# The experts' second layer with the weighted hidden values as stationary operand, in a vision tower on Trainium2

## What is computed

```python
logits = tokens @ router_w.T            # 8 experts
rw, re = top_k(softmax(logits), 2)      # two gates a token
rw = rw / rw.sum(-1)
out = tokens
for e in range(8):
    h = gelu(tokens @ w1[e] + b1[e])    # 64 -> 64
    y = h @ w2[e] + b2[e]               # 64 -> 64
    out = out + combine[:, e:e+1] * y
h = layernorm(out)
```

## Time and profile before

| | value |
|---|---|
| median of 3 runs | 2671.2 us |
| profiled execution | 2679.64 us, span 2677.9 us |
| TensorE matmul busy, whole span | 2344.8 us (88%) |
| VectorE | 1966.0 us (73%) |
| ScalarE | 1902.9 us (71%) |
| GpSimd | 1825.7 us (68%) |
| mean granted clock of TensorE | 0.97 |
| second stage | from about 2236 us to the end, 442 us |
| L1170 (down), matmuls | x512, 592 to 644 ns each |
| L1180 (turn_back), matmuls | x128, median 273 ns |

### The profile page before, as it was taken

One profiled execution on the slowest core, in us unless ns is written; L12 is line 12 of the kernel. 1 busy time (PEld: TensorE's weight loads), 2 busy tenths in 40 slices (PEclk: granted clock), 3 DMA queues, 4 the chain that ended last, 5 costly groups with the idle time before them and its releaser, 6 DMA issues. The chain is left out here.

```text
span 2677.9 us, 92863 instructions
## 1 busy us (share of the span) xinstructions
PE 2344.8 (88%) x32965; PEld 1114.5 (42%) x32965; DVE 1966.0 (73%) x4552; ACT 1902.9 (71%) x4717; POOL 1825.7 (68%) x1949
## 2 busy tenths in 40 slices
PE   1788888888888888888888888888888877999997
PEld 0344444444444444444444444444444443333332
DVE  4577777777777777777777777777777766898987
ACT  3777777777777777777777777777777764555554
POOL 3678877787787787777777877877877861222323
PEclk9999999999999999999999999999999996999999
DMA  4333333333333333333333333333332200000001
GB/s 83 73 65 65 65 65 65 64 65 64 65 65 65 64 65 65 64 65 65 65 65 64 65 65 64 65 65 62 67 65 60 54 2 1 21 20 20 20 21 27
DMA packets 573723, 147.95 MB, mean 55 GB/s; under 512 B 573440, under 2 KB 573440, under 8 KB 573440
## 3 DMA queue, kind: packets, MB, share of 16 engines
q1 hardware_dynamic: 573440, 143.52, 27.4%
HBM read 135.09 MB, written 8.39 MB: 54 GB/s over the span
## 5 line engine op out<-in xcount | busy, mean ns | idle before, releaser
L709 POOL TENSOR_TENSOR pv<-vs,aw 128x512 f32<-128x512 f32 x512 | 534.9, 1076 | 431.8 <-DVE aw L923 431.8
L840 DVE TENSOR_TENSOR kqs<-ps,qqT 128x512 f32<-128x512 f32 x512 | 352.0, 688 | 317.8 <-PE ps L390 313.9
L385 PE MATMUL ps<-xb,w_ckv 64*64 64x512 f32 x2048 | 570.4, 635 | 8.3 <-DVE kqs L840 5.1
L591 ACT ACTIVATE xd<-xb 128x512 f32<-128x512 f32 x512 | 576.1, 1151 | 0.0
L390 PE MATMUL ps<-xb,w_ckv 64*64 64x512 f32 x2048 | 570.6, 635 | 0.0
L573 ACT ACTIVATE sqs<-ps 128x512 f32<-128x512 f32 x512 | 309.5, 604 | 175.0 <-PE ps L390 174.9
L862 DVE TENSOR_REDUCE agg<-pv 128x128 f32<-128x1024 f32 x128 | 251.5, 1965 | 217.3 <-POOL pv L716 217.3
L486 PE MATMUL ps<-sm,vpad 128*32 128x128 f32 x4096 | 191.8, 284 | 197.2 <-DVE kqs L840 192.5
L753 POOL TENSOR_TENSOR xt<-xb 128x512 f32<-128x512 f32 x256 | 324.6, 1268 | 21.6 <-issue 21.2
L851 DVE TENSOR_TENSOR sm<-ps,decay 128x1024 f32<-128x1024 f32 x256 | 301.6, 1220 | 28.9 <-PE ps L467 28.1
L716 POOL TENSOR_TENSOR pv<-pv 128x512 f32<-128x512 f32 x256 | 321.8, 1278 | 0.0
(11 more groups left out here) (213 smaller groups left out, 4313.4 us busy)
## 6 DMA issues: line engine op xcount, KB each, us to landing
xb<-in_x_dram SPq DMA_DIRECT2D x512, 256.0 KB, 4.3
out_dram<-outb SPq DMA_DIRECT2D x128, 64.0 KB, 1.6
w1p<-in_L_ffn_w_dram SPq DMA_DIRECT2D x16, 16.0 KB
w2p<-in_L_ffn_w_dram SPq DMA_DIRECT2D x8, 16.0 KB
b1p<-in_L_ffn_b_dram SPq DMA_DIRECT2D x8, 0.2 KB
sm<-in_L_tok_Wkv_dram SPq DMA_DIRECT2D x4, 16.0 KB, 2.0
w_av<-in_L_attn_w_qkv_dram SPq DMA_DIRECT2D x4, 16.0 KB, 2.1
b2v<-in_L_ffn_b_dram SPq DMA_DIRECT2D x4, 2.0 KB
```

The source lines that it names most:

```text
L385: nc.tensor.matmul(KB[own, :], w_ckv[own, 2 * P + m * C:2 * P + (m + 1) * C], xv[own, j], start=True, stop=True)
L591: nc.scalar.activation(xd[:, j, :].rearrange("p (b t) -> p b t", b=ST), xb[:, f, :].rearrange("p (b t d) -> p d b t", b=ST, d=ST)[:, j], A ...
L709: nc.gpsimd.tensor_tensor(pv[:, at].rearrange("p (k d) -> p k d", d=D), vs[:, s, at].rearrange("p (k d) -> p k d", d=D), aw[:, j * W4:(j + ...
L840: V.tensor_tensor(kqs[:, j, :].rearrange("p (t d) -> p t d", d=ST), KB.rearrange("p (t d) -> p t d", d=ST), qqT[:, s, :].unsqueeze(2).to_b ...
```

## The change

In `down` the operands change places. For each half m and each block k of 128 tokens, hid[:, p, m, block] (128 x 128) is loaded and w2p[:, p, :] (64 columns) is streamed; the output has tokens on partitions, and the columns of YB are in the order of y. Per pair there are 8 written matmuls in place of 2. `bias2` is turned in the same way, 8 written f16 matmuls in place of 2, with the gates loaded and b2h or b2l streamed. `turn_back`, `turned`, yT and the semaphores ev_yt and tr_y fall away. `summed` writes y from YB itself and gives ev_y; it waits for y_done of three groups back, as `turned` did. `bias2` waits for ev_y in place of ev_yt, and `turn_tokens` no longer waits for ev_y.

```diff
--- before.py
+++ after.py
@@ -969,7 +969,6 @@
             tokT = sb2("tokT", [P, 4, 4 * P])
             cbT = sb2("cbT", [P, 2, 4 * P], F16)
             hid = sb2("hid", [P, 4, 2, 4 * P])
-            yT = sb2("yT", [P, 4 * P])
             y = sb2("y", [P, 2, 4 * P])
             y2 = sb2("y2", [P, 4 * P])
             nst = sb2("nst", [P, 4, 8])
@@ -995,8 +994,6 @@
             bc_done = sem("bc_done")
             hc_done = sem("hc_done")
             dn_done = sem("dn_done")
-            ev_yt = sem("ev_yt")
-            tr_y = sem("tr_y")
             ev_y = sem("ev_y")
             add_done = sem("add_done")
             sq_done = sem("sq_done")
@@ -1102,7 +1099,6 @@
                         pe.wait_ge(st_b, gdone(i, r, -2, 1))
                         pe.wait_ge(lg_done, gdone(i, r, -1, 1))
                         pe.wait_ge(ev_c, gdone(i, r, 0, 1))
-                        pe.wait_ge(ev_y, gdone(i, r, 2, 1))
                         for k in range(4):
                             mm = nc.tensor.transpose(TB[:, k * P:(k + 1) * P], st[:, r % 2, k * P:(k + 1) * P],
                                                      ident[:])
@@ -1155,30 +1151,23 @@
                 def bias2(i, r):
 
                     if gthere(i, r, 0):
-                        pe.wait_ge(ev_yt, gdone(i, r, 1, 1))
-                        nc.tensor.matmul(YB, b2h[0:64, :], cbT[0:64, r % 2, :], start=True, stop=False,
-                                         skip_group_check=True)
-                        nc.tensor.matmul(YB, b2l[0:64, :], cbT[0:64, r % 2, :], start=False, stop=False,
-                                         skip_group_check=True)
+                        pe.wait_ge(ev_y, gdone(i, r, 1, 1))
+                        for k in range(4):
+                            nc.tensor.matmul(YB[:, k * P:(k + 1) * P], cbT[0:64, r % 2, k * P:(k + 1) * P], b2h[0:64, :],
+                                             start=(k == 0), stop=False, skip_group_check=True)
+                            nc.tensor.matmul(YB[:, k * P:(k + 1) * P], cbT[0:64, r % 2, k * P:(k + 1) * P], b2l[0:64, :],
+                                             start=False, stop=False, skip_group_check=True)
 
                 def down(i, r, p, back=0):
 
                     if gthere(i, r, back):
                         pe.wait_ge(hc_done, gdone(i, r, back, 2 * NP, 2 * p + 2 - 2 * NP))
                         for m in range(2):
-                            h = slice(64 * m, 64 * m + 64)
-                            mm = nc.tensor.matmul(YB[h, :], w2p[:, p, :], hid[:, p, m, :], start=False,
-                                                  stop=(p == NP - 1), skip_group_check=True)
+                            for k in range(4):
+                                mm = nc.tensor.matmul(YB[:, (2 * k + m) * C:(2 * k + m + 1) * C],
+                                                      hid[:, p, m, k * P:(k + 1) * P], w2p[:, p, :], start=False,
+                                                      stop=(p == NP - 1), skip_group_check=True)
                         mm.then_inc(dn_done, 1)
-
-                def turn_back(i, r):
-
-                    if gthere(i, r, 1):
-                        pe.wait_ge(ev_c, gdone(i, r, -1, 1))
-                        pe.wait_ge(ev_yt, gdone(i, r, 1, 1))
-                        for k in range(4):
-                            mm = nc.tensor.transpose(TB[:, k * P:(k + 1) * P], yT[:, k * P:(k + 1) * P], ident[:])
-                        mm.then_inc(tr_y, 1)
 
                 def step(i, r):
                     up(i, r, 1)
@@ -1194,7 +1183,6 @@
                     turn_weights(i, r)
                     spread(i, r, 2)
                     down(i, r, 1)
-                    turn_back(i, r)
                     up(i, r, 0, 1)
                     spread(i, r, 3)
                     down(i, r, 2)
@@ -1243,15 +1231,8 @@
 
                     if gthere(i, r, 1):
                         act.wait_ge(dn_done, gdone(i, r, 1, NP))
-                        act.wait_ge(tr_y, gdone(i, r, 2, 1))
-                        nc.scalar.activation(yT[:], YB, ACT.Copy, scale=0.5).then_inc(ev_yt, 1)
-
-                def turned(i, r):
-
-                    if gthere(i, r, 1):
-                        act.wait_ge(tr_y, gdone(i, r, 1, 1))
                         act.wait_ge(y_done, gdone(i, r, 3, 1))
-                        nc.scalar.activation(y[:, 1 - r % 2, :], TB, ACT.Copy).then_inc(ev_y, 1)
+                        nc.scalar.activation(y[:, 1 - r % 2, :], YB, ACT.Copy, scale=0.5).then_inc(ev_y, 1)
 
                 def step(i, r):
                     gelu(i, r, 1)
@@ -1261,7 +1242,6 @@
                     logits(i, r)
                     gelu(i, r, 3)
                     weights(i, r)
-                    turned(i, r)
                     gelu(i, r, 0, 1)
                     halves(i, r)
                 groups(act, step)
```

## The result

The changed kernel takes 3104.5 us (median of 4 runs, 3099.12 to 3109.74); the kernel before took 2672.8 us beside it (4 runs, 2666.11 to 2674.68). The ratio is 1.162, with a 95% interval of 1.159 to 1.165. The time lies in the forecast's range of 2745 to 3185 us, 75 us above its 3030. The profiled execution took 3106.64 us, its span 3104.9.

What follows compares the result with a forecast made beforehand. TensorE's own order of blocks was taken as the bound: 3.72 + 0.07 - 0.68 - 0.5 = +2.6 us a group, +81 us over 31 groups to 2752, plus 282 for the low clock, 3034, rounded to 3030; range 2745 to 3185.

Steps and rivals of the forecast that it cites:

- The pace of down: Second stage, down: 16 load-paced pairs at 0.113 us, 1.94 us a block, 0.93 more; +3.72 us a group.
- Rival (d): Down's f32 loads run at 0.06 us a pair, 1.06 us a block; not slower, 2658 us; chance 0.03.
- rival (e): Down's loads and streams don't overlap in one array, 0.91 us more a block; 2865 us at full clock; chance 0.02.
- bias2: Second stage, bias2 block: 0.60 us as 8 f16 pairs in place of 0.53, +0.07 us a group.
- turn_back and the wait for VectorE: On TensorE, the four transposes with the wait ahead, and the wait at spread 3, go: -0.68 and -0.5 us a group.
- the -0.68: Per group on TensorE: four transposes (0.59 us) and the wait for ScalarE's gates copy ahead of them (0.09) go.
- the -0.5: Per group: TensorE's wait for VectorE at spread 3 goes, as longer down blocks let VectorE finish pair 2 by then.
- The sum at the full clock: Second stage: +2.6 us a group, 15.75 in place of 13.15; +81 us over 31 groups, 2752 us on the median.
- The clock: Second stage: the clock falls to half in the quiet stretch of logits, spread, bias2 and down 0; +14.1 us a low group.
- Rival (a): The clock stays full through the second stage, as TensorE is never idle; 2752 us; chance 0.22.
- How long it stays low: Second stage: clock falls within the first ten groups and is low in about 20 groups, 14.1 us each, +282 us.
- Waits that move: Second stage: bias2's wait for YB's copy stays covered, GpSimd's sum can start half a group sooner; all priced at nothing.

Runs made afterwards that it cites:

- reordered kernel: The changed kernel with up 3 moved ahead of bias2 and down 0, the same instructions in another order; 2743.3 us, ratio 1.030 to the kernel before.
- The last kernel above: Kernel before plus three filling matmuls per first-stage unit, GpSimd's token copy moved behind its scaling, and the square moved to ScalarE; 2633.6 us, ratio 0.986.
- without the way back: Kernel before without turn_back and the second copy, YB copied straight to y, output in wrong order; 2710.2 us, ratio 1.016.

## Why the prediction came out right, step by step

**The pace of down.** Forecast 1.94 us a block, from rows with 16 and 128 columns streamed; measured 1.93 with 64 columns, 1.98 with 128, 1.91 with 32. In these runs the load of 128 f32 columns is the pace, 1.93 / 16 = 0.12 us a pair with the tail. Rival (d), 1.06 us, and rival (e), 2.85, are out.

**bias2.** Forecast 0.60, measured 0.55 (2485.42 to 2485.97): +0.02 in place of +0.07.

**turn_back and the wait for VectorE.** Forecast gone, and gone: TensorE was busy 100% in each long stretch, at either clock, so the -0.68 and the -0.5 were both given.

**The sum at the full clock.** Forecast 15.75 us a group and +81 us. The reordered kernel, the nearest to a full-clock run of the change, has 15.60 us a group and 2743 us, 80 us over the kernel before beside it. Of the profiled executions only the second stage can be compared, since the first, with the same code, had 29, 24 and 21 falls of the clock. From its first logits block to the end of the span the second stage takes 2677.9 - 2238.15 = 439.8 us before, 516.4 in the reordered kernel and 877.9 in the kernel after:

```profile
2220.49 1.89 PE L1112 MATMUL ps<-rt,tokT 128*128 128x16 f32 x8 [0.75 <-ACT tokT L1199]
...
2227.00 1.89 PE L1112 MATMUL ps<-rt,tokT 128*128 128x16 f32 x8 [0.75 <-ACT tokT L1199]
```

(The first line is of the reordered kernel, span 2736.9 us, the second of the kernel after, span 3104.9.) So the full-clock part is +77 us, as 31 x (15.60 - 13.15) = 76 says, and the low clock +361. The sum needed three terms to hold at once; all three are seen one by one above. Its bounds were added up too wide: the terms' own bounds give 2748 to 2756, not 2744 to 2760.

**The clock.** The step that decided, and the one with the least behind it beforehand. Where it falls was as forecast, in down 0 behind logits, spread and bias2, or right at its end. That this is the cause and not a companion is shown twice: parting these blocks (2743) or filling down's streams (2759) takes the clock's part of the loss away, 361 and 346 us. Rival (a), at 0.22, had the rule of the Trainium skill ("TensorE: Matmul & The Clock Gate", Why this matters for your kernels) behind it, that the clock falls when TensorE idles and a loop without gaps stays at full; the trace contradicts it, with the clock at 0.50 and TensorE busy in all of 267.00 and 290.00 us.

**How long it stays low** was the mis-sized term. Forecast 20 groups at 14.1 us each, +282. Measured: a low group is 29.0 us, not 29.9, so 29.0 - 15.7 = 13.3; and the low time of 790 us is 790 / 29.0 = 27.2 groups' worth. 27.2 x 13.3 = 362 us, as the traces' second stages show (361). Against the forecast that is 7.2 groups more, +96 us; the price of the 20, -16; and the sum at the full clock, 77 in place of 81, -4: +76 us. The medians are 432 us apart where 363 was forecast, 69 more; the rest is in the first stage. The 20 groups were a judgement, with no row of such a loop for how long the clock would stay low; that the time came out 2.4% from the forecast owes something to luck. Two of its reasons need correcting. I had the clock fall "within the first ten groups": it fell in the first. And I tied its return to two up blocks in a row; that is how the stage's first return comes, but six later ones came behind a single up and the token turn, two behind a single up and the gates' turn. Why these returns stop at 2535, with the same blocks in the same order, stays open; the kernel with 32 columns has its last one at 2936.

**Waits that move.** "GpSimd's sum can start one half group sooner", priced at nothing, held only because TensorE had grown slower than all others. With a fast TensorE the same freedom costs 48 us of 2710, some 15 of them by the clock, and turns the gain of 16 to 22 that the removed work promised into a loss of 40. In the kernel after, VectorE and GpSimd collide too where the clock is full (L1286 at 2487.99 takes 0.69 us in place of 0.22), in the reordered kernel in most groups, but nobody waits for it: TensorE is busy throughout. In the long low part the group at 2822 shows no collision. The forecast's error there was of reasoning, not of size: an operation that is free to start sooner also starts beside other work.

So the change lost twice. Its price at the full clock is +80 us, 3%; the low clock adds 361. And its gain side, taken alone with the old down, was no gain either until GpSimd was held back, and then 9 us (2671.0 to 2662.3). The last kernel above keeps the transposes and takes 2629.9 - 2198.3 = 431.6 us for the second stage, 8 less than before.

## What to carry to other kernels

Before operands change places, count the columns loaded against the columns streamed: here an f32 block of 128-column loads with 32 to 128 columns streamed ran at the pace of the loads, and a row of such blocks took the clock down for hundreds of microseconds with TensorE at 100% busy. Look for stretches at 0.50 with a busy engine; the cure is not less work but another order, dense blocks between sparse ones, or filling matmuls where it waits anyway (361 us here, and 29 in the first stage). Look at the clock too where no sparse block was added: without the way back some 15 of the 48 us went that way, and no list of waits shows them. And a wait that falls away on GpSimd is to be priced by what VectorE does at the time when its work then starts.

## What the runs showed of the hardware that I had not expected

- With TensorE busy throughout, two states last: 1.00 for 495 us in the reordered kernel, and 0.50 for some 570 us in the kernel after, with the same instructions in orders that differ by one block.
- 16 pairs of a 128x128 f32 load and a stream take the same time with 32, 64 or 128 columns streamed, to within 4% (1.91, 1.93 and 1.98 us).
- At half the clock, blocks do not take quite twice their time: down 3.60 for 1.93, a group 29.0 for 15.7.
- Dummy matmuls made a kernel faster, by 1.0%.
- In a loop of dense blocks with 2.3 us of waits around spread 3 the clock fell for 3.4 us in every third group, which cost 1.55 us each time; with 0.9 us of waits at that place, in the kernel with GpSimd's sum held back, it never fell.
